# Ranks 9 and 10 sought in one list per head, the two sure pairs set aside, and the softmax's exponential as a power on GpSimd

## The reference

```python
s1, s2 = q1 @ K1.T, q2 @ K2.T                     # 64 scores each
v1, i1 = top_k(s1, 10);  v2, i2 = top_k(s2, 10)
all_scores = v1[:, None] + v2[None, :]            # 100 pair sums
vals, best = top_k(all_scores, 10)                # the 10 best pairs
expert = i1[best // 10] * 64 + i2[best % 10]
scores = softmax(vals)
h = gelu(x @ W_down[expert].T) * scores
out = h @ W_up[expert]
```

## Time and profile before

| | us |
|---|---|
| median of 3 runs | 3499.29 (3498.52 to 3501.48) |
| the profiled execution | 3501.89 |
| its span, first to last instruction | 3500.1 |
| busy in the span: PE, DVE, ACT, POOL | 3179.7, 2952.2, 2138.9, 1916.9 |
| mean granted TensorE clock | 0.897 of 2.4 GHz |

### The profile page before, as it was taken

The page is one execution under the profiler, slowest core; times in us unless marked ns, Lnnn a source line. Parts: engine busy times, 40 slices in busy tenths (PEclk is TensorE's granted clock), DMA queues, the critical chain, the costliest instruction groups (busy, mean ns, idle before and its releaser), DMA issues. The chain is left out here.

```text
span 3500.1 us, 91378 instructions
## 1 busy us (share of the span) xinstructions
PE 3179.7 (91%) x31284; PEld 2737.6 (78%) x31284; DVE 2952.2 (84%) x15052; ACT 2138.9 (61%) x4475; POOL 1916.9 (55%) x1758
## 2 busy tenths in 40 slices
PE   5999999982499999999999999999999999999998
PEld 3666666641388888888888888888888888888887
DVE  4566666655999999999999999999999999999942
ACT  3444444421677777766766776677667767776762
POOL 1333333332466666665556666666655566666652
PEclk9999999985699999999988899999999889999988
DMA  2111111103333333333333333333333333433332
GB/s 65 49 55 55 55 55 48 45 29 121 125 122 130 119 122 116 107 123 118 107 107 107 124 126 123 121 119 107 116 125 107 107 107 123 127 123 121 116 122 88
DMA packets 132329, 356.86 MB, mean 102 GB/s; under 512 B 13865, under 2 KB 61609, under 8 KB 129452
## 3 DMA queue, kind: packets, MB, share of 16 engines
q1 hardware_dynamic: 131868, 351.03, 31.0%
HBM read 309.01 MB, written 25.17 MB: 95 GB/s over the span
## 5 line engine op out<-in xcount | busy, mean ns | idle before, releaser
L1212 PE MATMUL b_ps_a<-b_wup,b_hid 128*128 128x256 f32 x4096 | 955.7, 379 | 0.0
L1201 PE MATMUL b_ps_h<-b_xT_hi,b_wd_split 128*128 128x256 f32 x4096 | 936.6, 313 | 19.6 <-ACT b_hid L1360 19.5
L1028 POOL TENSOR_TENSOR b_hid<-b_hid,b_gates 128x512 f32<-128x512 f32 x512 | 768.3, 1501 | 182.9 <-ACT b_hid L1360 182.5
L1212 PEld LDWEIGHTS b_ps_a<-b_wup,b_hid 128*128 128x128 f32 x4096 | 744.3, 190 | 84.0
L1201 PEld LDWEIGHTS b_ps_h<-b_xT_hi,b_wd_split 128*128 128x128 f32 x4096 | 707.2, 201 | 35.4 <-issue 24.9
L1339 ACT ACTIVATE b_ohq<-b_q_no,b_minus_qid 80x128 f16<-80x128 f16 x2048 | 648.4, 390 | 1.0
L1201 PE MATMUL b_ps_h<-b_xT_lo,b_wd_split 128*128 128x256 f32 x2048 | 598.9, 292 | 0.0
L1126 PE MATMUL b_ps_s<-b_ohr,b_ohq 80*128 80x32 f16 x16384 | 452.4, 185 | 106.9 <-issue 66.1
L1126 PEld LDWEIGHTS b_ps_s<-b_ohr,b_ohq 80*128 80x128 f16 x16384 | 443.6, 102 | 115.9 <-issue 72.3
L1360 ACT ACTIVATE b_hid<-b_ps_h 128x512 f32<-128x512 f32 x512 | 304.0, 594 | 372.2 <-PE b_ps_h L1201 372.2
L1043 POOL TENSOR_TENSOR b_ohq<-b_qT 80x640 f16<-80x640 f16 (+1 forms) x416 | 520.4, 1252 | 0.0
(11 more groups left out here) (195 smaller groups left out, 5484.6 us busy)
## 6 DMA issues: line engine op xcount, KB each, us to landing
b_wd_split<-wd_parts SPq DMA_DIRECT2D x512, 512.0 KB, 4.0
a_keysh<-a_key SPq DMA_DIRECT2D x16, 896.0 KB, 5.4
a_x<-in_x SPq DMA_DIRECT2D x16, 512.0 KB, 5.0
x_between<-a_y SPq DMA_DIRECT2D x16, 512.0 KB, 3.3
b_x<-x_between SPq DMA_DIRECT2D x32, 256.0 KB, 2.7
wd_parts<-b_wd_split SPq DMA_DIRECT2D x16, 512.0 KB, 3.0
b_x1t<-x_between SPq DMA_DIRECT2D x32, 256.0 KB, 5.5
out<-b_y SPq DMA_DIRECT2D x32, 256.0 KB, 5.4
```

Source lines behind the costliest of these rows:

```text
L1028: G.tensor_tensor(hid[:, p % 4, :, :], hid[:, p % 4, :, :], gates[:, 2 * p:2 * p + 2, :], ALU.mult).then_inc(mix_done, 1)
L1201: mm = T.matmul(hbank[p % 2][:, j * C:(j + 1) * C], a, c, start=i == 0, stop=i == len(parts) - 1)
L1212: mm = T.matmul(abank[:, t * D:(t + 1) * D], hid[:, p % 4, j, t * P:(t + 1) * P], wup[:, 2 * p + j, :], start=p == 0 and j == 0 and t == 0 ...
```

## The change

Four things change in the expert phase.

1. `lists_first` runs for both tiles, then a new `choose` decides for each head which of its two lists can hold a rank beyond 8 that matters, and copies that list's scores and its best 8 over the first list's (two COPY_PREDICATED). `lists_rest` then searches 8 lists per tile instead of 16. `place_rest` puts the found ranks 9 and 10 in place, and a very small number in the list that was not searched.
2. `sure_pairs` sets aside the two pairs that are always among the ten: (0, 0), and the larger of (0, 1) and (1, 0). `pairs_top` then needs only the best 8 of the rest, two steps instead of five.
3. The exponential leaves ACT: `soften` there is gone, with its two table loads and the dummy gelu. POOL gets `exponentials`, one TENSOR_TENSOR of 128 partitions x 160 elements that raises e to each element.
4. `numbers` and `pair_sums` wait for the new steps, and the semaphore counts follow.

```diff
@@ pool_program
+        def exponentials(m):
+            g4 = gate[:, :, :].rearrange("p t s -> p (t s)")
+            pool.wait_ge(half_set, 1)
+            pool.wait_ge(shift_done, m + 1)
+            G.tensor_tensor(g4, base_e[:, :].to_broadcast([P, NT * SLOTS]), g4, ALU.pow).then_inc(exp_done, 1)
...
             if has(m + 3):
                 low_x(m + 3)
+            if has(m + 2):
+                exponentials(m + 2)
             if has(m):
                 root(1, m)
                 add_input(m)
@@ act_program
-        def soften(m):
-            g4 = gate[:, :, :].rearrange("p t (h k) -> p (t h) k", k=TOPK)
-            act.wait_ge(shift_done, m + 1)
-            S.activation(g4, g4, ACT.Exp).then_inc(exp_done, 1)
-
-            act.wait_ge(half_set, 1)
-            S.activation(unused[:, :], gelu_in[:, :], ACT.Gelu)
@@ dve_program
+        def choose(m):
+            v = val.rearrange("p t (h s) k -> p (t h) s k", s=2)
+            s = score.rearrange("p t (h s) n -> p (t h) s n", s=2)
...
+            V.tensor_copy(v[:, :, 0, 8:16], v[:, :, 0, 0:8])
+            V.tensor_tensor(ends[:, :, 0], v[:, :, 0, 0], v[:, :, 1, 2], ALU.add)
+            V.tensor_tensor(ends[:, :, 1], v[:, :, 0, 7], v[:, :, 1, 0], ALU.add).then_inc(choice_done, 1)
...
+            V.copy_predicated(v[:, :, 0, 8:16], second.unsqueeze(2).to_broadcast([P, NT * HEADS, 8]), v[:, :, 1, 0:8])
+            V.copy_predicated(s[:, :, 0, :], second.unsqueeze(2).to_broadcast([P, NT * HEADS, NSQ]),
+                              s[:, :, 1, :]).then_inc(choice_done, 1)
+
         def lists_rest(m, t):
-            src = lambda l: score[:, t, l, :]
-            dve.wait_ge(lists_done[t], 5 * m + 2)
-            for l in range(LISTS):
-                op = V.match_replace(src(l), val[:, t, l, 0:8], src(l), GONE)
+            src = lambda h: score[:, t, 2 * h, :]
+            dve.wait_ge(choice_done, 4 * m + 3)
+            for h in range(HEADS):
+                op = V.match_replace(src(h), val[:, t, 2 * h, 8:16], src(h), GONE)
...
+        def sure_pairs(m):
+            first, either = cand[:, :, 0:1], cand[:, :, 1:11:9]
...
         def pairs_top(m, t):
...
-            for h in range(HEADS):
-                op = V.match_replace(src(h), vals(h)[:, 0:8], src(h), GONE)
-            op.then_inc(pairs_done[t], 1)
-            dve.wait_ge(pairs_done[t], 5 * m + 3)
-            for h in range(HEADS):
-                op = V.max(vals(h)[:, 8:16], src(h))
...
```

More of the change, by code:

```diff
@@ L39 @@
 NQ_ACT = NQ
+SURE = 8
 CA = 512
@@ L831, in experts_phase @@
     cand = sb("b_cand", [P, NT * HEADS, NPAIR], F32)
+    ends, absent, second = cand[:, :, 0:2], cand[:, :, 2:4], cand[:, :, 4].bitcast(mybir.dt.uint32)
     cid = sb("b_cid", [P, HEADS, NPAIR, NT], F16)
@@ L1389, in act_program @@
                 scores(m + 3)
-            if has(m + 2):
-                soften(m + 2)
             if has(m + 1):
@@ L1515, in lists_rest @@
             dve.wait_ge(lists_done[t], 5 * m + 3)
-            for l in range(LISTS):
-                op = V.max(val[:, t, l, 8:16], src(l))
+            for h in range(HEADS):
+                op = V.max(val[:, t, 2 * h + 1, 8:16], src(h))
             op.then_inc(lists_done[t], 1)
             dve.wait_ge(lists_done[t], 5 * m + 4)
-            for l in range(LISTS):
-                op = V.max_index(idx[:, t, l, 8:16], val[:, t, l, 8:16], src(l))
+            for h in range(HEADS):
+                op = V.max_index(idx[:, t, 2 * h + 1, 8:16], val[:, t, 2 * h + 1, 8:16], src(h))
@@ L1522, in lists_rest, with place_rest @@
             op.then_inc(lists_done[t], 1)
+        def place_rest(m):
+            v = val.rearrange("p t (h s) k -> p (t h) s k", s=2)
+            i = idx.rearrange("p t (h s) k -> p (t h) s k", s=2)
+            for t in range(NT):
+                dve.wait_ge(lists_done[t], 5 * m + 5)
+            V.tensor_copy(i[:, :, 0, 8:TOPK], i[:, :, 1, 8:TOPK])
+            for s in range(2):
+                op = V.scalar_tensor_tensor(v[:, :, s, 8:TOPK], absent[:, :, s:s + 1].to_broadcast([P, NT * HEADS, TOPK - 8]), GONE,
+                                            v[:, :, 1, 8:TOPK], ALU.mult, ALU.add)
+            op.then_inc(choice_done, 1)
@@ L1543, in pair_sums @@
             op.then_inc(cand_done, 1)
+        def sure_pairs(m):
+            first, either = cand[:, :, 0:1], cand[:, :, 1:11:9]
+            s01, s10 = cand[:, :, 1:2], cand[:, :, 10:11]
+            dve.wait_ge(cand_done, m + 1)
+            V.tensor_tensor(won[:, :, 0:1], s01, s10, ALU.is_ge)
+            V.tensor_tensor(won[:, :, 1:2], s01, s10, ALU.is_lt)
+            V.tensor_copy(top[:, :, SURE:SURE + 1], first)
+            V.tensor_tensor(top[:, :, SURE + 1:TOPK], s01, s10, ALU.max).then_inc(sure_done, 1)
+            dve.wait_ge(sure_done, 2 * m + 1)
+            V.memset(first, GONE)
+            V.tensor_scalar(posf[:, :, :].rearrange("p (h k) t -> p t h k", k=TOPK)[:, :, :, SURE + 1],
+                            won[:, :, 0].rearrange("p (t h) -> p t h", t=NT), -9.0, 10.0, ALU.mult, ALU.add)
+            V.scalar_tensor_tensor(either, won[:, :, :], GONE, either, ALU.mult, ALU.add).then_inc(sure_done, 1)
         def pairs_top(m, t):
@@ L1618, in dve_program @@
                 lists_first(m + 2, 0)
-            if has(m + 2):
+                lists_first(m + 2, 1)
+                choose(m + 2)
                 lists_rest(m + 2, 0)
-                lists_first(m + 2, 1)
                 lists_rest(m + 2, 1)
+                place_rest(m + 2)
                 pair_sums(m + 2)
+                sure_pairs(m + 2)
                 pairs_top(m + 2, 0)
```

45 lines of the change are left out of this document (24 added, 21 removed).

## The result

| | us |
|---|---|
| before, median | 3499.44 (3498.52 to 3501.48) |
| after, median | 3733.66 (3724.56 to 3737.2) |
| ratio, 95% interval | 1.0662 (1.0648 to 1.0677) |
| the profiled execution of after, its span | 3724.56, 3722.8 |

The change makes the kernel 234 us slower; the forecast was 3682, that is 183 us slower. The direction, the cause and most of the size held. One step did not, and about 48 us hang on it.

What follows compares the result with a forecast made beforehand. It took the pass tail to be a PE-DVE chain that POOL's 25.2 us power would delay by 6.1 us in 30 passes (+183 us), with nothing for the search or ACT's saving: 3682 us, range 3450 to 3770.

Steps and rivals of the forecast that it cites:

- What bounds a pass: PE's three gate-matrix stops: 1.32 us for ACT, then 0.55 and 0.96 us in a chain between PE and DVE.
- Part 3, the power's length: POOL's power over 160 elements: 25.2 us, straight on from powers of 2 and 4 elements; chance 0.57.
- rival A: POOL's power is cheap in bulk, up to 17.8 us: 3458 us, or 3384 with a clock gain; chance 0.31, 0.06 with clock.
- C: POOL's power is dearer, 33.5 us, 8.3 us more a pass: 3931 us; chance 0.07.
- Part 3, the threshold: On POOL between `low_x` and the root, a power of up to 17.8 us costs nothing.
- Part 3, +6.1 us a pass: Power on POOL delays root, `norm_out`, block 3's rows and PE's block 3: +6.1 us in 30 passes, +183 us.
- Part 2, -41 us: ACT's four instructions (3.06 us) go, removing PE's 1.32 us stop in 31 passes; not added beside the long power.
- Part 1, the search 10 us shorter and worth 0: DVE's search: 15.4 us removed, 4 to 5 us of small instructions added, net 10 us less, worth 0 on the path.
- rival D: Earlier DVE work collides with POOL's mixes; if PE stood still 1 us a pass, 31 us more in any case.
- Behind that point the change takes nothing off its work: DVE already idles 1.93 us for PE at block 0, and its work after that is not reduced: worth 0.
- The opening: Three opening passes: 5 us gained on DVE, cancelled by `soften` waiting for a slow power; 0.
- The clock: First 4.8 us of a pass run at the lower clock and stay so: nothing added, a microsecond a pass allowed.

Runs made afterwards that it cites:

- Experiment 3: Kernel before with ACT's `soften` moved from behind the score copies to ahead of `queries`: 3458.85 us, 0.9883 of the kernel before.
- 8: Kernel before with the new search, `choose` operands in PSUM, ACT's exponential ahead of `queries`, `norm_out` behind block 3's rows: 3417.52 us, 0.9756.
- 10: Kernel before with the new search, `choose` operands in PSUM, ACT's exponential ahead of `queries`, `norm_out` in its old place: 3435.51 us, 0.9817.
- experiment 5: Kernel before plus six POOL powers of 8 to 320 elements ahead of the expert phase: 1.65 to 51.32 us each, 3593.57 us in all.
- experiment 9: Kernel before with the exponential on POOL over only the first tile's 80 elements, the second tile's left out: 3453.53 us, 0.9861.
- experiment 11: Changed kernel, power still on POOL, with one end sum and the mask of `choose` in PSUM: 3685.38 us, 1.0536 of the kernel before.
- experiment 2: Kernel before with the exponential moved from ACT to POOL and the old search kept: 3713.99 us, 1.061 of the kernel before.
- experiment 6: Changed kernel with the exponential back on ACT, and one end sum and the mask of `choose` in PSUM: 3482.75 us, 0.9943.
- experiment 4: Changed kernel with the exponential back on ACT and POOL's mixes and one-hot products replaced by memsets: 3479.55 us, single run.

## Why the prediction was right, and where it was not

- **What bounds a pass: right.** The stops at the gate matrix were read as a chain from PE's block 0 over DVE's rows, `norm_out` and DVE's rows to PE's block 3, with a first stop that is ACT's. Experiment 3 takes away ACT's and leaves the chain; 8 against 10 takes `norm_out` out of it and gains 0.9 us in most passes, its 0.91.
- **Part 3, the power's length: right.** 25.2 us forecast from powers of 2 and 4 elements, 25.85 measured. The choice between a straight line, a bend and a dearer growth was the one on which all hung, and experiment 5 shows the line up to 320 elements. The argument for it (so long a calculation per element leaves little overhead to spread) was right in its result. Rivals A and C fall with it. The estimate of 0.35 us by the Trainium skill's pace for a two-input elementwise instruction (GPSIMD Engine Reference, section 3.1) isn't met where the operation is a power.
- **Part 3, the threshold: right as far as tried.** Up to 17.8 us were to be free; 13.13 us are (experiment 9), 25.85 cost 6 us a pass. Between them nothing was run.
- **Part 3, +6.1 us a pass: right with nothing else in the way.** 86.3 us forecast, 86.45 in experiment 11, 86.9 in experiment 2 (the old search). That experiment 11 comes so near is partly luck. The power is 0.65 us longer than forecast, which is experiment 2's 86.9; experiment 11 gets most of it back because its last two mixes are shorter (2.41 and 2.66 us for 2.99 and 3.24) and the power starts 0.4 us earlier in the pass.
- **Part 2, -41 us: right, and rightly not added.** Alone it gives -41 (experiment 3), or -47 in experiment 9. Beside the long power, experiment 2's passes show nothing of it. The further gain by the clock, which rival A thought possible, didn't come in either.
- **Part 1, the search 10 us shorter and worth 0: wrong.** This is the step that failed: "Added are 16 small instructions and two COPY_PREDICATED; the small ones of the trace take about 0.3 us (the reduction in the earlier trace rows), so 4 to 5 us at most". The search became 8 us longer. `choose` was mis-sized: 16.65 us where the same instructions beside a quiet POOL take some 2.4 (0.18 us each for the small ones, 0.31 and 1.36 for the predicated copies), 14 us more. Behind it, `shift` with the casts went from 2046.83 - 2046.23 = 0.6 to 2058.72 - 2053.56 = 5.2 us for the same reason, and `mask` with `product` from 5.7 to 7.3. Together some 20 us of waits; without these the search would have been 12 us shorter. And a late search had a second way to the path that the sum left out: `numbers` on POOL waits for it, and the power stands behind `numbers`. The sum had the power begin where `low_x` ended before.
- **Why it was missed.** The rule of two SBUF inputs was in the prediction, under rival D. But it was asked only how much the *long* DVE instructions slow POOL or wait for a power, and not how long the *short* ones wait for the mixes. The sum took its 0.3 us from a reduction, which has one input. The kernel before already showed the other case: `pair_sums` (five additions of two lists) took 2.00 us beside the mixes, and takes 1.18 in the changed kernel, where POOL waits for it.
- **"Behind that point the change takes nothing off its work", worth 0: half right.** A gain on DVE is indeed worth nothing in a steady pass (experiment 6: 80.2 us). A loss is worth something as soon as it is larger than DVE's spare time: the sum had no term for that side, only D's 1 us a pass for a PE that waits for the mixes.
- **The opening: near enough.** It was put at 0. The first `norm_out` starts at 1030.58 us before, at 1033.69 in the changed kernel and at 1025.61 in experiment 11. Without the power it gains more: experiment 6 has it at 1013.62.
- **The clock.** Over the steady stretch from 1500 to 3200 us the granted clock falls from 0.90 to 0.87, in the row of the changed kernel (columns as in the earlier trace rows). The forecast added nothing for it, and experiment 11, with 0.878 over its span, still comes within 4 us of the sum.

```profile
1500.00:3200.00 1700.00, 1490.30 (x17010) 1372.44 (x17010) 1648.26 (x5661) 1040.61 (x2355) 1433.93 (x920) 0.87 0.33 106
```

## What to carry to other kernels

Before pricing a small DVE instruction, look at how many SBUF inputs it has and what POOL does at that time; beside a POOL that works without a gap, 16 elements cost 1.3 to 2.6 us, not 0.2, and one operand in PSUM gives them back. Ask as well which other engine waits for the late instruction, and what stands behind that wait. Before moving work to an idle engine, work out how long its idle window is up to the next thing on that engine that others wait for, and price the operation itself there (a power is 159 ns an element on POOL), not its kind. A gain on an engine with spare time is worth nothing, but a loss on it counts from the point where the spare time ends, so a sum needs both sides.

## What the hardware showed that was not expected

- DVE waits for POOL and hardly the other way round, as long as DVE's instructions are short: the mixes and one-hot products beside `choose` keep their 1.26 to 1.30 us. Only beside the larger COPY_PREDICATED one mix took 1.78.
- The power does not hold up DVE. `product`, with two SBUF inputs, ran at 2063.73 in its 2.41 us, wholly inside the power's 2060.97 to 2086.83, and faster than the 3.37 us it took beside a mix. Over the 32 passes its median is 2.41. The Trainium skill's rule, as the prediction cites it (SBUF — State Buffer, "Who interferes with whom"), that the two exclude each other for the whole of an instruction, doesn't agree with this: it fits the mixes, not the power. Whether any DVE instruction slows a power can't be seen; its length varies by only 16 ns over 32 of them.
- Copies wait too: the COPY of 128 elements took 2.05 us for 0.32 in experiment 4, and two CASTs, 0.32 us before, took 2.60 us.
- A power costs 0.4 us and 0.159 us for each element of a partition, from 8 to 320 elements.
